# Splitting the down projection of every expert into high and low parts: six reduced-precision products in place of two full ones

## The reference

```
x = layernorm(x + attention(x))          # 16 heads, decaying running sums, w_qkv 512x1536, w_out 512x512
scores = softmax(x @ gate_w.T)           # 64 experts, 6 chosen for a row, at most 128 rows for an expert
gu  = einsum('ech,ehi->eci', gx, gate_up_proj)      # per expert: 128x512 @ 512x384
g, u = split(gu);  hid = silu(g) * u                # 128x192
eo  = einsum('eci,eih->ech', hid, down_proj) * buf_w  # 128x192 @ 192x512
x = layernorm(x + scatter_add(eo) + shared_expert(x))
```

## Time and profile before

| | |
|---|---|
| Median of 3 runs | 973.73 us (968.06 to 974.46) |
| The profiled execution | 971.29 us, its span 969.4 us |
| PE busy | 944.1 us (97%) |
| DVE, ACT, POOL busy | 685.0, 502.4 and 464.6 us |
| Granted clock of TensorE, mean | 0.989 |

### The profile page before, as it was taken

One profiled execution on the slowest core, in us unless ns is written; L12 is line 12 of the kernel. 1 busy time (PEld: TensorE's weight loads), 2 busy tenths in 40 slices (PEclk: granted clock), 3 DMA queues, 4 the chain that ended last, 5 costly groups with the idle time before them and its releaser, 6 DMA issues. The chain is left out here.

```text
span 969.4 us, 15236 instructions
## 1 busy us (share of the span) xinstructions
PE 944.1 (97%) x4658; PEld 757.1 (78%) x4658; DVE 685.0 (71%) x1251; ACT 502.4 (52%) x1015; POOL 464.6 (48%) x543
## 2 busy tenths in 40 slices
PE   8999999999999999999999999999999999998996
PEld 7888888888888888877887777767777777767875
DVE  7977787969778796887766565655666665635776
ACT  5532444434343434534447565656565675534775
POOL 4002264555655555587234446454455554432564
PEclk9999999999999999989999999999999999999998
DMA  6343442434252433356558999999999999959963
GB/s 202 99 141 109 146 123 96 128 125 120 80 170 86 138 105 124 101 173 210 169 194 250 317 328 312 305 306 306 324 327 323 312 315 306 321 96 383 376 252 118
DMA packets 114191, 203.93 MB, mean 210 GB/s; under 512 B 18496, under 2 KB 56384, under 8 KB 113088
## 3 DMA queue, kind: packets, MB, share of 16 engines
q1 hardware_dynamic: 93584, 159.87, 49.5%
q0 software_dynamic: 19520, 35.75, 16.1%
q10 hardware_dynamic: 1008, 7.34, 2.0%
HBM read 143.03 MB, written 59.88 MB: 209 GB/s over the span
## 5 line engine op out<-in xcount | busy, mean ns | idle before, releaser
L1511 POOL DMA_INDIRECT slot_table<-tokens,slot_of x162 | 179.4, 1107 | 112.1 <-issue 59.7
L1553 POOL DMA_INDIRECT acc_rows<-eo,table_sb x64 | 111.0, 1734 | 172.7 <-ACT eo L879 138.3
L1608 PE MATMUL bank<-x_hi,wqkv_hi 128*128 128x512 f32 x384 | 153.4, 399 | 1.2 <-DVE wqkv_lo L963 1.1
L1608 PE MATMUL bank<-x_hi,wqkv_lo 128*128 128x512 f32 x384 | 150.7, 393 | 0.0
L1608 PE MATMUL bank<-x_lo,wqkv_hi 128*128 128x512 f32 x384 | 150.4, 392 | 0.0
L1376 DVE TENSOR_TENSOR wgu_lo<-wgu,wgu_hi 128x1536 fp32r<-128x1536 f32 x64 | 112.5, 1759 | 43.2 <-ACT wgu_hi L873 43.2
L1608 PE MATMUL bank<-wdn,hid_et 96*128 96x512 f32 x256 | 122.4, 600 | 6.2 <-ACT hid_et L915 6.1
L873 ACT CAST wgu_hi<-wgu 128x1536 fp32r<-128x1536 f32 x64 | 94.5, 1477 | 1.1 <-DMA wgu<-w_gu 0.5
L1542 POOL DMA_INDIRECT xg<-x_rows,table_sb x64 | 74.3, 1161 | 42.1 <-DVE table_sb L1111 22.8
L1608 PE MATMUL bank<-wgu_hi,xgt_hi 128*128 128x384 f32 x256 | 91.4, 357 | 0.0
L647 ACT ACTIVATE e<-bank 128x512 f32<-128x512 f32 x64 | 38.0, 593 | 97.4 <-PE bank L1608 97.4
(11 more groups left out here) (179 smaller groups left out, 2213.4 us busy)
## 6 DMA issues: line engine op xcount, KB each, us to landing
wgu<-w_gu SPq DMA_DIRECT2D x64, 768.0 KB, 8.1
wdn<-w_down SPq DMA_DIRECT2D x64, 384.0 KB, 8.3
xres<-x SPq DMA_DIRECT2D x32, 256.0 KB, 3.0
x_turned<-x1t SPq DMA_DIRECT2D x32, 256.0 KB, 2.7
x_rows<-x SPq DMA_DIRECT2D x32, 256.0 KB, 3.0
acc_rows<-x SPq DMA_DIRECT2D x32, 256.0 KB, 3.0
fin<-acc_rows SPq DMA_DIRECT2D x8, 1024.0 KB, 12.2
odd<-acc_rows SPq DMA_DIRECT2D x8, 1024.0 KB, 13.5
```

Of the source, the lines that this page charges most:

```text
L1511: pool.indirect_dma_start(table_dram, bass.IndirectOffsetOnAxis(slot_of[:, i, k:k + 1], 0), tokens[:, i:i + 1], None, bounds_check=SLOTS - ...
L1553: pool.indirect_dma_start(acc_dram[e % 2], bass.IndirectOffsetOnAxis(table_sb[:, e:e + 1], 0), eo[eo_slot[e]][:, :], None, bounds_check=T ...
L1608: mm = pe.matmul(out_ap, a, b, start=first and i == 0, stop=final and i == len(products) - 1)
```

## The change

The down product is made of two-part numbers as well. `SPLIT = 2` says how many of the two halves of the 192 hidden columns are split: both. In each iteration:

- ACT gets `split_down(e + 1)`, a copy of 96x1024 of the down weights into `wdn_hi`, placed behind `scale_rows(e - 1)` and ahead of the unit and of the copy of the turned hidden rows. The copy of the hidden rows writes `hid_et_hi` in the rounded type; its size is unchanged.
- DVE gets `split_down(e + 1)`, the 96x1024 subtraction into `wdn_lo` (over the weights themselves), behind `wgu_lo` and ahead of the unit; and `split_hidden(e - 1)`, a 96x256 subtraction out of the bank `ht_ps`, as the first instruction of the iteration.
- PE does six products in place of two in `down`, and waits there for `wdn_lo` and `hid_et_lo`; its hidden transposes wait for `hid_et_lo` of the expert before, and no longer for `hid_et`.

The loads keep their conditions. The new tiles lie in memory that was free.

```
+            def split_down(e):                                   # ACT
+                act.wait_ge(dn_in[e % ND], 16 * (e // ND + 1))
+                if e >= 2:
+                    act.wait_ge(eo_mm, e - 1)
+                act.copy(wdn_hi[e % 2][:, :, :], wdn_buf[e % ND][:, 0:SPLIT, :]).then_inc(wdn_hi_done, 1)
...
                 if e:
                     scale_rows(e - 1)
+                if e + 1 < NE:
+                    split_down(e + 1)
                 for _ in range(fills_of[e]):
                     unit()
                 act.wait_ge(ht_mm, e + 1)
...
-                act.copy(hid_et[e % 2][:, :, :], ht_ps[0:IH, 0:2 * P].rearrange("p (h s) -> p h s", h=2)).then_inc(hid_et_done, 1)
+                act.copy(hid_et_hi[e % 2][:, :, :], turned[:, 0:SPLIT, :]).then_inc(hid_et_done, 1)
...
+            def split_down(e):                                   # DVE
+                dve.wait_ge(wdn_hi_done, e + 1)
+                dve.tensor_tensor(wdn_lo[e % ND][:, :, :], wdn_buf[e % ND][:, 0:SPLIT, :], wdn_hi[e % 2][:, :, :].bitcast(F32),
+                                  ALU.subtract).then_inc(wdn_lo_done, 1)
+
+            def split_hidden(e):
+                dve.wait_ge(hid_et_done, e + 1)
...
+                dve.tensor_tensor(hid_et_lo[e % 2][:, :, :], turned[:, 0:SPLIT, :], hid_et_hi[e % 2][:, :, :].bitcast(F32),
+                                  ALU.subtract).then_inc(hid_et_lo_done, 1)
...
+                if e:
+                    split_hidden(e - 1)
                 dve.wait_ge(tanh_e_done, e + 1)
...
                 if e + 2 < NE:
                     split_expert(e + 2)
+                if e + 1 < NE:
+                    split_down(e + 1)
...
             def down(e):
-                pe.wait_ge(hid_et_done, e + 1)
                 pe.wait_ge(dn_in[e % ND], 16 * (e // ND + 1))
                 if e:
                     pe.wait_ge(eo_done, e)
-                chain(eo_ps[:, :], [(hid_et[e % 2][:, k, :], wdn_buf[e % ND][:, k, :]) for k in range(2)]).then_inc(eo_mm, 1)
+                pe.wait_ge(wdn_lo_done, e + 1)
+                pe.wait_ge(hid_et_lo_done, e + 1)
...
+                for h in range(SPLIT):
+                    products += three(hid_et_hi[e % 2][:, h, :], hid_et_lo[e % 2][:, h, :], wdn_hi[e % 2][:, h, :], wdn_lo[e % ND][:, h, :])
+                chain(eo_ps[:, :], products).then_inc(eo_mm, 1)
...
                 if e:
-                    pe.wait_ge(hid_et_done, e)
+                    pe.wait_ge(hid_et_lo_done, e)
```

More of the change, by code:

```diff
@@ L89, in build @@
     wgu_buf = [both.place(f"wgu{i}", [P, KC, GU]) for i in range(2)]
+    wdn_at = [both.at + 4 * i * 2 * D for i in range(2)]
     wdn_buf = [both.place(f"wdn{i}", [IH, 2, D]) for i in range(2)]
+    SPLIT = 2
     att = Map(nc, both.at, end)
@@ L192, in build @@
     wgu_lo = [Map(nc, at, at + 4 * KC * GU).place(f"wgu_lo{i}", [P, KC, GU], F32R) for i, at in enumerate(wgu_at)]
+    wdn_at += [late.at + 4 * i * 2 * D for i in range(ND - 2)]
     wdn_buf += [late.place(f"wdn{i}", [IH, 2, D]) for i in range(2, ND)]
+    wdn_lo = [Map(nc, at, at + 4 * SPLIT * D).place(f"wdn_lo{i}", [IH, SPLIT, D], F32R) for i, at in enumerate(wdn_at)]
     assert late.at <= projected_end + 8 * 4 * BT
@@ L206, in build @@
     hid_e = [late.place(f"hid_e{i}", [P, I]) for i in range(2)]
-    hid_et = [late.place(f"hid_et{i}", [IH, 2, P]) for i in range(2)]
+    hid_et_hi = [late.place(f"hid_et_hi{i}", [IH, SPLIT, P], F32R) for i in range(2)]
+    hid_et_rest = [late.place(f"hid_et_rest{i}", [IH, 2 - SPLIT, P]) for i in range(2)] if SPLIT < 2 else []
     assert late.at <= kept_from
@@ L212, in build @@
     xg += [late.place(f"xg{i}", [P, D + E]) for i in range(NXG - 2, NXG)]
+    wdn_hi = [late.place(f"wdn_hi{i}", [IH, SPLIT, D], F32R) for i in range(2)]
+    hid_et_lo = [late.place(f"hid_et_lo{i}", [IH, SPLIT, P], F32R) for i in range(2)]
     fin_map = Map(nc, both.at - 2 * 4 * (KC * GU + 2 * D), both.at)
@@ L358, in build @@
             sem("xgt_hi_done"), sem("wgu_hi_done"), sem("tanh_e_done"), sem("hid_et_done"), sem("eo_done"))
+        wdn_hi_done, wdn_lo_done, hid_et_lo_done = sem("wdn_hi_done"), sem("wdn_lo_done"), sem("hid_et_lo_done")
         stage_lo, x_lo_first, decay_done = sem("stage_lo"), sem("x_lo_first"), sem("decay_done")
@@ L896, in _ @@
             split_rows(0)
+            split_down(0)
             for _ in range(BEFORE_EXPERTS[2]):
@@ L914, in _ @@
                     act.wait_ge(eo_mm, e - 1)
-                act.copy(hid_et[e % 2][:, :, :], ht_ps[0:IH, 0:2 * P].rearrange("p (h s) -> p h s", h=2)).then_inc(hid_et_done, 1)
+                turned = ht_ps[0:IH, 0:2 * P].rearrange("p (h s) -> p h s", h=2)
+                if SPLIT < 2:
+                    act.copy(hid_et_rest[e % 2][:, :, :], turned[:, SPLIT:2, :])
+                act.copy(hid_et_hi[e % 2][:, :, :], turned[:, 0:SPLIT, :]).then_inc(hid_et_done, 1)
             scale_rows(NE - 1)
@@ L1377, in split_expert @@
                                   ALU.subtract).then_inc(wgu_lo_done, 1)
+            def split_down(e):
[4 more added lines that the diff above has]
+                dve.wait_ge(hid_et_done, e + 1)
+                if e >= 2:
+                    dve.wait_ge(eo_mm, e - 1)
+                turned = ht_ps[0:IH, 0:2 * P].rearrange("p (h s) -> p h s", h=2)
+                dve.tensor_tensor(hid_et_lo[e % 2][:, :, :], turned[:, 0:SPLIT, :], hid_et_hi[e % 2][:, :, :].bitcast(F32),
+                                  ALU.subtract).then_inc(hid_et_lo_done, 1)
             for _ in range(BEFORE_EXPERTS[0]):
@@ L1413, in _ @@
                     split_expert(e + 2)
+                if e + 1 < NE:
+                    split_down(e + 1)
                 for _ in range(fills_of[e]):
                     unit()
+            split_hidden(NE - 1)
             added = 0
@@ L1851, in down @@
                     pe.wait_ge(eo_done, e)
-                chain(eo_ps[:, :], [(hid_et[e % 2][:, k, :], wdn_buf[e % ND][:, k, :]) for k in range(2)]).then_inc(eo_mm, 1)
+                pe.wait_ge(wdn_lo_done, e + 1)
+                pe.wait_ge(hid_et_lo_done, e + 1)
+                products = [(hid_et_rest[e % 2][:, h - SPLIT, :], wdn_buf[e % ND][:, h, :]) for h in range(SPLIT, 2)]
+                for h in range(SPLIT):
+                    products += three(hid_et_hi[e % 2][:, h, :], hid_et_lo[e % 2][:, h, :], wdn_hi[e % 2][:, h, :], wdn_lo[e % ND][:, h, :])
+                chain(eo_ps[:, :], products).then_inc(eo_mm, 1)
             for _ in range(BEFORE_EXPERTS[0]):
```

## The result

The changed kernel takes 1018.7 us (median of 4 runs, 1012.4 to 1023.5) beside 974.1 us before: the ratio is 1.0456, with a 95% interval of 1.0416 to 1.0496, so 44 us or 4.6% slower. The forecast was +33 us, 1006, in a range of 972 to 1055. The profiled execution took 1014.15 us, 42.9 more than that of before. The four executions differ by 11 us, and the mean granted clock of TensorE goes with them: 0.985 and 0.983 at 1012.4 and 1014.2 us, 0.977 and 0.973 at 1023.3 and 1023.5.

The account below looks back on a forecast made before the run. PE was taken to bound the expert stage, with DVE setting iterations without a unit after the change. PE's gain -8, DVE's pace +14 and the load +27 made +33 us: 1004 profiled, 1006 for a median, range 972 to 1055.

Parts of the forecast that it names:

- DVE's term: Expert stage: DVE sets 42 iterations without a unit at 4.8 us against 4.46, +14 us; +6 with PE's -8.
- The load: ACT's down-weight copy waits for a load landing in 6.8 us; 21 iterations at 1.3 us, +27 us.
- Prices of the instructions: Weight copy 1.05 us, weight subtraction 1.22, hidden subtraction 0.42; six products 1.36 us in place of 1.72.
- PE stays the bound there and its gain of 0.36 is real: Iterations with a unit: PE needs 7.24 us, more than DVE; 22 times -0.36 us, -8 us.
- F: Iteration with a unit on PE, which runs during the load's wait; that wait was to cost nothing.
- N2: Iteration without a unit, 4.8 us, load needed after 5.5 us; nothing hides a later landing, +27 us over 21.
- N1 at 4.8: Iteration without a unit, at DVE's pace of 4.8 us; its load has 7.9 us, reaching across a unit.
- The loop of 4.74 us: Chain through ACT's and DVE's lists from one down product to the next, 4.74 us before hand-offs.
- The scatter-add wait at 0: ACT's waits in `scale_rows`, 34.7 us in 17, mostly hidden: 0 us more, at worst 34.7.
- Rival A: Expert stage: DVE catches up during the unit and PE's whole 23 us come, 951 us; chance 0.13.
- Rival C: TensorE's clock falls after gaps, at worst 36 us more, about 1042; chance 0.15, shared with a landing near the median.
- Rival B: Down loads land in under 5.5 us, so no change: 977 us profiled, 980 by the median; chance 0.17.

Follow-up runs that it names:

- run 1: Changed kernel with a fourth buffer for the down weights, each load issued one iteration earlier; 1002.3 us, ratio 1.0301 to the kernel before.
- run 12: Changed kernel without the gathers of rows for experts 6 to 63; 1003.4 us, ratio 1.0306 to the kernel before.
- run 5: Changed kernel with ACT's down-weight copy moved behind its hidden-row copy and DVE's weight subtraction moved into the next iteration; 981.1 us, ratio 1.0029 to before.
- run 11: Changed kernel without down-weight copy and subtraction after the first two experts, and without gathers for experts 6 to 63; 952.6 us, ratio 0.977 to before.
- run 4: Changed kernel with six products but neither copy nor subtraction of the down weights after the first two experts; 972.6 us, ratio 1.0007 to before.
- run 10: Kernel before the change without the gathers of rows for experts 6 to 63; 963.6 us, ratio 0.9879 to the kernel before.
- run 8: Kernel before the change with ACT's scatter-add wait corrected to the expert whose buffer is taken; 984.4 us, ratio 1.007 to before.

## Why the prediction was right, and where it was not

The direction, the main chain (PE waits for `hid_et_lo`, DVE for ACT, ACT for the load) and the size (44 us against 33) were right, the range held. The terms of the sum were less so, and that it came near is in part luck: DVE's term was over 20 us too small and the load's 12 too large.

- *Prices of the instructions*: `wdn_lo` 1.22 forecast and 1.221 measured, `wdn_hi` 1.05 and 1.043, the hidden subtraction 0.42 and 0.41, six products from 621.52 to 622.99, 1.47 us with the slower start of the first, against 1.36. PE's gain per iteration is 0.33 (4.46 to 4.13), forecast 0.36.
- *"PE stays the bound there and its gain of 0.36 is real" (F)*. This failed. Forecast for F was 0.36 us less than before, which by the table would be 6.88 us; measured 7.75. (The prediction's own figure is 7.24. It counted a unit at 3.14 us, but a unit adds 7.24 - 4.46 = 2.8: it begins while the last matmul of the down product still runs. With 2.8, and 4.1 for the long one, the sum by which the prediction closed is some 347 us and not 355; the rest of the 356 are PE's waits of 6.1 us and a stretch at the lower clock, so that sum closed by luck.) I compared DVE's work with PE's over the iteration, but the down product stands ahead of the unit and must wait for what DVE is late with from N2. Around one unit PE needs 3 x 4.10 us besides it and DVE 3 x 4.78 = 14.3; measured 17.5 - 2.8 = 14.7. The unit is added on top of DVE's pace. This is the step that was mis-sized: DVE's place and pace cost 27 to 30 us (27 by the table with four buffers, 29 and 30 by the ratios of runs 1 and 12), where I had +6.
- *N1 at 4.8*: measured 4.13, N2 5.6. PE has its down product in N1 without a gap, and what DVE is behind shows in N2 and F.
- *The loop of 4.74 us* was read rightly as what ties DVE to PE; run 5 loosens it, fills the 0.68 us and wins 42 us. The earlier trace rows show this idle time, and the sum did not use it.
- *The load*: 15 us (run 1), where I had 27. Its landing came to 6.5 us in the median, forecast 6.8, and ACT waited 26.3 us. But N2 did not feel it: there DVE is late anyway. It was paid mostly in two F iterations, of 15.8 and 13.9 us, and F I had at nothing.
- *The scatter-add wait at 0*: 3.1 us in one wait, but that one was half of the longest stall.
- *Rival A (PE's 23 us come)* had its stated condition, a loop shorter than 4.46 us, met in run 5, and still did not come. There it was DVE for the most part: F, N1 and N2 are 16.1 us together where PE alone needs 15.2 (4.13 twice and 6.95 in run 11), 19 us over 21 such groups. With DVE's weight subtraction gone (run 4) the DMA engines were a second bound just behind PE, as runs 10 and 11 show for half of the gain. The row with the DMA engines always at work stood in the prediction, and it was used for the landing alone. It is no proof by itself: 107 MB at 301 GB/s give 356 us in any case, since the rate is these bytes divided by this time.
- *Rival C (the clock)* came only in small part. In the profiled execution the mean granted clock went from 0.989 to 0.983, and the lower level cost about 6 us in the stage; the two executions at 1023 us had 0.977 and 0.973. The clock fell in or right behind three of the 50 gaps, those of 6.1, 4.6 and 2.7 us, and behind none of the other 47, of 1.9 us and less, 41 us in all; yet the earlier trace rows show it fallen behind one of 1.89 us. The Trainium skill ("TensorE: Matmul & The Clock Gate", "HAM oscillation — how this bites in real kernels") describes a loop that drops to half rate on every pass, in which the matmuls of a pass take less time than the DMA wait behind them. The prediction took this kernel for such a loop; here 4 us and more of matmuls stand between gaps of mostly 1.2 us or less, and it was not one.
- *Rival B (no change)* would have needed the load in time; run 1 had that and still was at 1.03.

## What to carry to other kernels

Before a helper engine is given more work, ask which instruction of the main engine waits for it and what stands behind that instruction: cover that comes after the wait hides nothing. Put the new step where the helper already idles and away from the hand-off of the same iteration, and do so before changing its size; here two moved calls were worth 42 us, and halving the added work 19. When the main engine is 98% busy, ask what stands right behind it before making it faster: here six cheaper products won nothing alone, and half of what they save with 17% less traffic. That the DMA engines always have work does not tell whether they bind (their share hardly fell with less traffic); taking traffic away does. And shorter waits on one transfer can turn into waits on another.

## What the runs showed of the hardware

With one wait on another semaphore (run 8) ACT's 34.7 us of waiting for the scatter-add went, and 60.3 us of waiting for gate/up loads came. The mix of weight loads, gathers and scatter-adds moved 301 GB/s from 509 to 865 us in before and 302 in runs 4 and 5. Whether that is a ceiling of the mix is not shown: these kernels move the same bytes in nearly the same time, and one slice of the page of before, in its last stage, shows 383 GB/s. With a sixth of the traffic gone the DMA engines still had work 0.97 of the time, at 268 GB/s.

After gaps of 6.1, 4.6 and 2.7 us in PE's work the granted clock was 0.50, the lower level, where the earlier trace rows show it after a gap of 1.89 us; after 47 other gaps of up to 1.9 us it stayed up. A gap in PE's timeline is worth more than its figure: iterations with one are 0.2 to 0.3 us longer than their gap and their work. Without a wait the down product starts 0.03 us after the start of the last transpose, which lasts 0.27 us (run 11), and a gap is counted only from that end.
